# Last attention stage of a 16-batch kernel: scores in two row halves, value masks on ScalarE, and residual additions on GpSimd

## The reference

```
q = norm(x) @ c_Wq + c_bq                  # 256 rows, 16 heads of 8
k = o @ c_Wk + c_bk;  v = o @ c_Wv + c_bv  # o: the 16 slots of the batch
a = softmax(q k^T / sqrt(8))               # for each head: 256 x 16
out = x + (a v) @ c_Wo + c_bo              # heads side by side, then c_Wo
```

## Time and profile before

| | |
|---|---|
| median of 3 runs | 196.59 us (196.57 to 197.86) |
| profiled execution | 196.71 us, its span 195.2 us |
| busy in the span | PE 179.0, DVE 140.9, ACT 118.2, POOL 147.7 us |
| last stage | about 145.6 to 195.2 us |
| granted clock of PE | 1.00 of full |

### The profile page before, as it was taken

How to read it: one execution, slowest core, us unless ns; L and a number is a source line. 1 busy time by engine, 2 the same in 40 slices (tenths; PEclk the granted TensorE clock), 3 DMA queues, 4 the chain that set the end, 5 groups by cost and what they waited for, 6 DMA issues and landing times.

```text
span 195.2 us, 4705 instructions
## 1 busy us (share of the span) xinstructions
PE 179.0 (92%) x1439; PEld 136.3 (70%) x1439; DVE 140.9 (72%) x409; ACT 118.2 (61%) x297; POOL 147.7 (76%) x289
## 2 busy tenths in 40 slices
PE   0588899999999999999999999999977799999994
PEld 0525577778877778777878776623656599999993
DVE  1468978898869786977676652555536999999971
ACT  1323467796889778778767676535412466665661
POOL 4898877899988965969478591306947999999970
PEclk9999999999999999999999999999999999999999
DMA  3749948999980000000000000000000001111122
GB/s 91 240 150 367 349 120 321 331 380 317 382 212 3 0 2 3 3 0 3 0 3 0 2 5 0 3 0 0 3 0 0 3 27 54 57 57 44 42 81 81
DMA packets 19658, 18.24 MB, mean 93 GB/s; under 512 B 1273, under 2 KB 15442, under 8 KB 19634
## 3 DMA queue, kind: packets, MB, share of 16 engines
q1 hardware_dynamic: 18130, 16.76, 26.8%
q10 hardware_dynamic: 1504, 1.18, 1.9%
HBM read 15.84 MB, written 2.10 MB: 92 GB/s over the span
## 4 chain that ended last, share of the span: by engine, by line
PE 82%; DVE 6%; POOL 5%; issue 2%; DMA 1%; ACT 1%; ACTq 1%; DVEq 0%
PE ps L1006 15%; PE ps L1262 7%; PE ps L1076 6%; PE ps L1235 6%; PE ps L1121 4%; PE ps L1179 4%; PE ps L1016 4%; PE ps L1252 4%; PE ps L1109 4%; PE ps L1059 3%; PE ps L1039 3%; PE ps L1243 3%; PE ps L1029 3%; PE ps L1049 2%; PE ps L1068 2%
## 5 line engine op out<-in xcount | busy, mean ns | idle before, releaser
L1006 PE MATMUL ps<-Wproj,xnT 128*128 128x512 f32 x64 | 32.3, 629 | 1.7 <-ACT xnT L559 0.8
L463 POOL TENSOR_TENSOR pr<-ft,rsm 128x256 f32<-128x256 f32 x32 | 19.3, 625 | 0.9 <-DVE rsm L922 0.9
L1006 PEld LDWEIGHTS ps<-Wproj,xnT 128*128 128x128 f32 x64 | 11.5, 199 | 10.7 <-issue 9.4
L1235 PE MATMUL ps<-xnT,XN2T 128*128 128x256 f32 x64 | 16.5, 383 | 1.8 <-POOL xnT L470 1.0
L631 ACT ACTIVATE ft<-ex 128x512 f32<-128x512 f32 x16 | 10.1, 630 | 12.0 <-POOL pr L463 7.1
L1262 PE MATMUL ps<-sq,prT 128*128 128x128 f32 x128 | 16.8, 275 | 0.0
L751 DVE TENSOR_REDUCE ss<-sq 128x64 f32<-128x512 f32 x16 | 10.8, 678 | 8.1 <-ACT sq L535 7.9
L1076 PE MATMUL ps<-XN2T,Ad 128*128 128x256 f32 x64 | 16.6, 382 | 0.0
L411 POOL TENSOR_SCALAR xn<-X,nm,rs 128x127 f32<-128x127 f32 x32 | 14.7, 469 | 1.7
L528 ACT ACTIVATE pr<-ps,nmax 128x256 f32<-128x256 f32 x32 | 14.9, 472 | 1.7 <-DVE nmax L790 1.6
L379 POOL TENSOR_SCALAR xn<-X,nm,rs 128x127 f32<-128x127 f32 x32 | 14.9, 477 | 1.1 <-PE ps L1039 0.9
(11 more groups left out here) (173 smaller groups left out, 510.4 us busy)
## 6 DMA issues: line engine op xcount, KB each, us to landing
W1s<-in_L_ffn_e_W_dram SPq DMA_DIRECT2D x4, 1024.0 KB, 8.2
Wgs<-in_L_ffn_e_Wg_dram SPq DMA_DIRECT2D x4, 1024.0 KB, 8.7
W2s<-in_L_ffn_e_W_dram SPq DMA_DIRECT2D x16, 256.0 KB, 8.3
out_dram<-V2s SPq DMA_DIRECT2D x16, 128.0 KB, 1.7
X<-in_L_attn_x_dram SPq DMA_DIRECT2D x2, 512.0 KB, 6.6
X<-in_L_attn_x_dram ACTq DMA_DIRECT2D x1, 512.0 KB, 7.1
X<-in_L_attn_x_dram ACTq DMA_DIRECT2D x1, 384.0 KB, 5.9
X<-in_L_attn_x_dram ACTq DMA_DIRECT2D x1, 128.0 KB, 2.4
```

Source lines behind the costliest of these rows:

```text
L463: last = pool.tensor_tensor(heads(at[:, k, j * HS:(j + 1) * HS], S), heads(ep[:, k, j * HS:(j + 1) * HS], S), over(rsm[:, k, j * H:(j + 1) ...
L1006: last = pe.matmul(ps[:, j, :], xnT[:, k, j * P:(j + 1) * P], Wproj[:, :], start=True, stop=True)
L1235: last = pe.matmul(ps[:, 2 + k, j * HS:(j + 1) * HS], XN2T[:, b, j * P:(j + 1) * P], BDk[:, k, :], start=True, stop=True)
```

## The change

The masked keys have 128 columns in place of 256: rows 0 to 63 hold heads 0 to 7 and rows 64 to 127 hold heads 8 to 15, in the same columns. The scores of a half of the rows are then two products, each over 64 rows and 128 columns, into two banks, which DVE reads in one view. The four banks of scores leave one for the turned weights, one for the value product (both had two) and two for the output.

The values' mask leaves POOL. ACT reads the value product of all batches out of PSUM once for each head, with the head's column of the mask as scale and the masked bias, and writes that head's columns of BDv for all 16 batches (which lies now in the space of expert weights that are used up). Eight of these 16 instructions stand ahead of `step2`, four behind the exponential of batch 0, four behind that of batch 1. PE waits for all 16 before the first value product.

For the batches 0, 1, 2, 4, 5, 6, 8, 9, 10 and 12 (`BY_POOL`) ACT copies the output from PSUM to `ob` one step after PE made it, between its exponential and its `atT`, and POOL adds the rows, between its `at` and its BDk. The other six stay with DVE. SP waits for POOL's or DVE's semaphore by batch.

```diff
+BANK_TT, BANK_VW, BANK_OUT = 4, 6, (5, 7)
+
+BY_POOL = tuple(int(b % 4 != 3 and b < NB - 3) for b in range(NB))
...
-        BDv = qm[:, :, 0:HS]
+        BDv = W1s[:, 0:8, :].rearrange("p e f -> p (e f)").rearrange("p (b m) -> p b m", b=NB)
...
+        def scored(k):
+
+            return ps[:, 2 * k:2 * k + 2, 0:NT].rearrange("p r (g s) -> p r g s", s=S)
...
             def step2(t):
-                if live(t, 5):
-                    b, k = of(t, 5)
-                    wait(pool, vwp_ok, b - 1)
-                    pool.tensor_tensor(heads(BDv[:, k, :], S), under(vT[:, :, b], H), over(head8[:, :], S),
-                                       ALU.mult).then_inc(bdv_ok, 1)
                 if live(t, 6):
...
                     last.then_inc(at_ok, 1)
+                if live(t, 8) and BY_POOL[t - 8]:
+                    b, k = of(t, 8)
+                    wait(pool, kept_ok, sum(BY_POOL[:b + 1]))
+                    pool.tensor_tensor(ob[:, k, :], ob[:, k, :], X[:, b, :], ALU.add).then_inc(obp_ok, 1)
                 if live(t, 1):
                     b, k = of(t, 1)
                     wait(pool, sp_ok, b - 1)
-                    pool.tensor_tensor(heads(BDk[:, k, :], S), under(kT[:, :, b], H), over(head8[:, :], S),
+                    pool.tensor_tensor(heads(BDk[:, k, 0:P], S), under(kT[:, :, b], H // 2), over(head8c[:, :], S),
                                        ALU.mult).then_inc(bdk_ok, 1)
...
+            def head_values(h):
+
+                sc.activation(BDv[:, :, h * S:(h + 1) * S], ps[:, 5, 0:2 * P].rearrange("p (s b) -> p b s", b=NB),
+                              ACT.Identity, bias=bcv8[:, h:h + 1], scale=head8[:, h:h + 1]).then_inc(bdv_ok, 1)
+
             sc.wait_ge(kvp_ok, 4)
-            sc.activation(vT[:, :, :].rearrange("p s b -> p (s b)"), ps[:, 5, 0:2 * P], ACT.Identity,
-                          bias=vecT[:, BCV:BCV + 1]).then_inc(vT_ok, 1)
+            for h in range(8):
+                head_values(h)
...
                     sc.activation(ep[:, k, :], sx[:, k, :], ACT.Exp).then_inc(ep_ok, 1)
+                    if b < 2:
+                        for h in range(8 + 4 * b, 12 + 4 * b):
+                            head_values(h)
+                if live(t, 7) and BY_POOL[t - 7]:
+                    b, k = of(t, 7)
+                    wait(sc, op_ok, b + 1)
+                    wait(sc, stored[k], (b // 2) * 16, NB * 8)
+                    sc.activation(ob[:, k, :], ps[:, BANK_OUT[k], 0:NT], ACT.Copy).then_inc(kept_ok, 1)
                 if live(t, 5):
...
+                ve.tensor_tensor(head8c[:, :], head8[:, 0:H // 2], head8[:, H // 2:H], ALU.add)
+                ve.tensor_scalar(bcv8[:, :], head8[:, :], vecT[:, BCV:BCV + 1], None, ALU.mult)
...
-                if live(t, 5):
+                if live(t, 5) and not BY_POOL[t - 5]:
...
                     for j in range(2):
-                        last = pe.matmul(ps[:, 2 + k, j * HS:(j + 1) * HS], XN2T[:, b, j * P:(j + 1) * P],
-                                         BDk[:, k, :], start=True, stop=True)
+                        for r in range(2):
+                            rows8 = slice(r * 64, r * 64 + 64)
+                            last = pe.matmul(ps[:, 2 * k + r, j * P:(j + 1) * P], XN2T[rows8, b, j * P:(j + 1) * P],
+                                             BDk[rows8, k, 0:P], start=True, stop=True)
                     last.then_inc(sp_ok, 1)
                 if live(t, 4):
                     b, k = of(t, 4)
-                    wait(pe, bdv_ok, b + 1)
-                    wait(pe, vw_ok, b - 1)
+                    wait(pe, bdv_ok, H)
+                    wait(pe, vw_ok, b)
...
                     wait(pe, at_ok, b + 1)
-                    wait(pe, atT_ok, b - 1)
+                    wait(pe, atT_ok, b)
...
-                    wait(pe, ob_ok, b - 1)
+                    if b >= 2 and BY_POOL[b - 2]:
+                        pe.wait_ge(kept_ok, sum(BY_POOL[:b - 1]))
+                    elif b >= 2:
+                        pe.wait_ge(ob_ok, (b - 1) - sum(BY_POOL[:b - 1]))
```

More of the change, by code:

```diff
@@ L111, in build @@
         head4 = sb("head4", P, EG)
+        head8c = sb("head8c", P, H // 2)
+        bcv8 = sb("bcv8", P, H)
         heads64 = sb("heads64", P, P // 2)
@@ L229, in build @@
         ta_ok, actT_ok, y_ok, o2s_ok, to_ok = (sem(n) for n in ("ta_ok", "actT_ok", "y_ok", "o2s_ok", "to_ok"))
-        o2_ok, kvp_ok, kT_ok, vT_ok = (sem(n) for n in ("o2_ok", "kvp_ok", "kT_ok", "vT_ok"))
+        o2_ok, kvp_ok, kT_ok = (sem(n) for n in ("o2_ok", "kvp_ok", "kT_ok"))
         stored = [sem("stored0"), sem("stored1")]
@@ L291, in _ @@
             for b in range(NB):
-                sp.wait_ge(ob_ok, b + 1)
+                if BY_POOL[b]:
+                    sp.wait_ge(obp_ok, sum(BY_POOL[:b + 1]))
+                else:
+                    sp.wait_ge(ob_ok, b + 1 - sum(BY_POOL[:b + 1]))
                 sp.dma_start(out_rows[:, b, :], ob[:, b % 2, :]).then_inc(stored[b % 2], 16)
@@ L469, in step2 @@
                     wait(pool, sp_ok, b - 1)
-                    pool.tensor_tensor(heads(BDk[:, k, :], S), under(kT[:, :, b], H), over(head8[:, :], S),
+                    pool.tensor_tensor(heads(BDk[:, k, 0:P], S), under(kT[:, :, b], H // 2), over(head8c[:, :], S),
                                        ALU.mult).then_inc(bdk_ok, 1)
             pool.wait_ge(kT_ok, 2)
-            for t in range(STEPS2):
-                if t == 5:
-                    pool.wait_ge(vT_ok, 1)
+            for t in range(STEPS2 + 1):
                 step2(t)
@@ L641, in step2 @@
                     wait(sc, op_ok, b - 1)
-                    sc.activation(VWs[:, k, :], ps[:, 1 - k, 0:HS], ACT.Copy).then_inc(vw_ok, 1)
+                    sc.activation(VWs[:, k, :], ps[:, BANK_VW, 0:HS], ACT.Copy).then_inc(vw_ok, 1)
             for t in range(STEPS2):
@@ L911, in step2 @@
                     wait(ve, ep_ok, b - 1)
-                    ve.tensor_tensor(heads(sx[:, k, :], S), heads(ps[:, 2 + k, :], S), over(mx[:, k, :], S),
-                                     ALU.subtract).then_inc(sx_ok, 1)
+                    ve.tensor_tensor(sx[:, k, :].rearrange("p (r g s) -> p r g s", r=2, s=S), scored(k),
+                                     mx[:, k, :].rearrange("p (r g) -> p r g", r=2).unsqueeze(3)
+                                     .broadcast_to([P, 2, H, S]), ALU.subtract).then_inc(sx_ok, 1)
                 if live(t, 2):
@@ L930, in step2 @@
                     wait(ve, sp_ok, b + 1)
-                    ve.tensor_reduce(mx[:, k, :], heads(ps[:, 2 + k, :], S), AX.X, ALU.max).then_inc(mx_ok, 1)
+                    ve.tensor_reduce(mx[:, k, :].rearrange("p (r g) -> p r g", r=2), scored(k), AX.X,
+                                     ALU.max).then_inc(mx_ok, 1)
             ve.wait_ge(xcbo_ok, NB)
@@ L1239, in step2 @@
                     b, k = of(t, 4)
-                    wait(pe, bdv_ok, b + 1)
-                    wait(pe, vw_ok, b - 1)
+                    wait(pe, bdv_ok, H)
+                    wait(pe, vw_ok, b)
                     for hf in range(2):
-                        last = pe.matmul(ps[:, 1 - k, hf * P:(hf + 1) * P], BDv[:, k, hf * P:(hf + 1) * P],
+                        last = pe.matmul(ps[:, BANK_VW, hf * P:(hf + 1) * P], BDv[:, b, hf * P:(hf + 1) * P],
                                          W[:, CO, :], start=True, stop=True)
@@ L1248, in step2 @@
                     wait(pe, at_ok, b + 1)
-                    wait(pe, atT_ok, b - 1)
+                    wait(pe, atT_ok, b)
                     for j in range(2):
                         for hf in range(2):
-                            last = pe.transpose(ps[:, 4 + k, hf * NT + j * P:hf * NT + (j + 1) * P],
-                                                at[:, k, j * HS + hf * P:j * HS + (hf + 1) * P], ident[:, :])
+                            last = pe.transpose(ps[:, BANK_TT, hf * NT + j * P:hf * NT + (j + 1) * P],
+                                                at[:, k, hf * HS + j * P:hf * HS + (j + 1) * P], ident[:, :])
                     last.then_inc(tt_ok, 1)
```

10 lines of the change are left out of this document (5 added, 5 removed).

## The result

The changed kernel takes 207.73 us (median of 4 runs, 206.63 to 208.9) against 196.99 for the kernel before: a ratio of 1.055 (95% interval 1.050 to 1.060). It is slower, by 10.7 us, and it lies 1.4 us above the top of the forecast range. The executed profile took 208.57 us, with a span of 206.9.

What follows compares the result with a forecast made beforehand. PE bounds the last stage now; a ring of POOL and ACT waits would bound it after. Start, rings and tail put the last weights' end at 196.2 for 189.79: 196.71 + 6.4 = 203.1 us (203.0 against the median), range 200.5 to 206.3.

Steps and rivals of the forecast that it cites:

- The sign: Whole kernel: slower, by +6.4 us; chances slower 0.88, same 0.10, faster 0.02.
- Rival (1): Last stage: PE keeps the pace because the waits have slack; 197.2 us, not measurably slower; chance 0.08.
- The ring: Last stage: POOL's addition waits for ACT's exponential and copy, which wait for POOL's weights; 3.40 us a batch; chance 0.70.
- the start: Stage's beginning: sixteen ACT value masks delay the first value product to 153.2 from 150.34; batch 3's weights end at 162.1.
- The high end of the range: 206.3 us: value masks at 0.474 (+1.1), the circle of waits at 3.55 (+1.35), scores not side by side (+0.9).
- Side by side: PE's 64-row score products run in pairs at once, 0.43 us a batch instead of 0.86 one after the other.
- 0.31 a round trip: PE's scores: entering and leaving the tiled shape costs 0.31 us a batch, making scores 0.74 for 0.86.
- a step of 2.52: PE's time per batch in the last stage, with scores at 0.74: 2.52 us for 2.64.
- The one bank of values: Single value-product bank: costs later steps nothing; the last two batches wait 0.45 us each, 0.9 in the tail.
- its rivals: PE-paced cases charged 0.9 us at the tail: 197.2 us (chance 0.08), or 195.5 with free shape changes (0.05).

Runs made afterwards that it cites:

- e2: Changed kernel with POOL's output addition one POOL step later, behind the next batch's weights; 203.70 us, ratio 1.028.
- e5: Changed kernel with ACT's copy of the output moved ahead of its exponential in the same step; 204.64 us, ratio 1.035.
- e6: Kernel before with only ACT's output copies and POOL's additions for the same ten batches put in; 212.86 us, ratio 1.075.
- e3: Changed kernel with five unused products on PE ahead of its wait for the value masks; 206.28 us, ratio 1.041.
- e10: Scores-only kernel (64-row scores, new banks, half key mask) with the eight score instructions made twice; 203.96 us, ratio 1.029 to the kernel before.
- e4: Changed kernel with values masked per batch by POOL and all additions on DVE, as before; 198.42 us, ratio 0.999 to the kernel before.
- e1: Changed kernel with all sixteen output additions on DVE and no output copy on ACT; 205.31 us, ratio 1.035.
- e9: Changed kernel with POOL's addition one step later and five unused products keeping PE busy before the value masks; 202.03 us, ratio 1.023.
- e7: Kernel before with only ACT's value masks, head by head for all batches, replacing POOL's value mask; 201.09 us, ratio 1.018.
- e8: Scores-only kernel with the value product over 64 rows too, its halves in two banks, one output bank; 198.70 us, ratio 1.006.

## Why the prediction was right in its cause and too low

**The sign and the mechanism held.** Rival (1), PE keeps the pace, is out: POOL's wait is in all ten rounds. The ring was put at 3.40 and is 3.36; piece by piece, the hand-over to ACT is 0.08 (0.08 forecast), exponential to copy 0.54 (0.54), the addition's duration 0.73 (0.73), the key mask's 0.465 (0.47). e2 and e5 open it from either end without moving work between engines, and e6 builds it in the other kernel at the size of the sum. From the end of A(3) to the end of A(15) the profile has 201.54 - 167.06 = 34.5 us, the forecast 34.1.

**What failed is the step called the start.** It said that A(3) would end 16.5 us into the stage (162.1 - 145.6); it ended 19.9 into it (167.06 - 147.15), 3.4 later. Two things made that up.

First, a term that was not in the sum: the clock. The text lets PE wait for the masks until 153.2 and then counts the value product at 0.45 and the scores at 0.74. After 4.65 us without an instruction PE had the level of 1.2 GHz, and they took 1.22 and 1.18. e3 gives its price, 2.3 us: there A(3) ends 17.6 us into the stage. How long the low level lasts behind the wait differs from one execution to the next, so this price does too (e2). The profile before shows a clock of 1.00 in the whole stage; I took that for a property of the stage, and it belonged to a PE that hardly waits.

Secondly, a term that was mis-sized: a value mask takes 0.47 start to start (3.75 for eight), not 0.40. The new instruction lasts longer than the L622 that I took, 0.599 us mean for 0.474:

```profile
L634 ACT ACTIVATE W1s<-ps,bcv,head 128x256 f32<-128x256 f32 x16 | 7.7, 599 | 3.9 <-PE ps L1242 3.9
```

It differs in two things, the scale from memory and the strides, and no run separates them. Over sixteen the value product came 8.48 us into the stage for 7.6, 0.9 late. The two terms make 3.2 of the 3.4 us.

The high end of the range had the masks at 0.474, but nothing for the clock. The rest of the distance is no fault of the mechanism. A(5) to A(7) and A(9) to A(11) took 5.27 each for 5.17, and A(8) to A(9) 3.64 for 3.40 (the exponential waits for DVE there), 0.4 over all steps. And the profiled execution's stage began 1.55 later than that of before, for the most part ahead of the change's first instruction, as said above. The sum, 3.4 + 0.4 + 1.55, is about the 5.5 us between the 208.57 of the profile and the 203.1 forecast for it.

**The scores.** "Side by side" held (e10). "0.31 a round trip" was too small: it is 0.42, and with 0.44 for the products the two terms add up to the 0.86 of before, so this part of the change gains nothing (e4: ratio 0.999). I had said 0.12 a batch, a step of 2.52 for PE where e1 has 2.64. In the changed kernel the ring hides the difference. The Trainium skill says in "TensorEngine Tiling (Array Packing)", Key Properties, that changing the tiling mode drains TensorE. The trace agrees, with about 0.2 us for each change of shape.

**The one bank of values** costs the steady steps nothing, as said. For each of the last two batches it costs 0.6 of waiting rather than 0.45, and the value product takes 0.23 more, 1.7 us in all where the text had 0.9 (e4). The text charged it to its rivals only; in the changed kernel the ring hides it.

**The sum as the runs have it.** The two parts of the stage (us, one profile each):

| kernel | first part | second part |
|---|---|---|
| before | 11.77 | 34.97 |
| changed | 16.26 | 40.68 |
| e1, no additions on POOL | 16.48 | 36.65 |
| e2, additions late | 15.60 | 36.64 |
| e3, PE kept busy | 13.98 | 40.70 |
| e4, scores and banks alone | 10.45 | 36.64 |
| e9, e2 and e3 together | 14.00 | 36.65 |

Of 10.2 us the ring is 4.0 (40.68 - 36.65), the half clock 2.3 (16.26 - 13.98), the later value product, less what the shorter masks and scores give back, 2.2 (14.00 - 11.77), and the one bank at the end 1.7 (36.65 - 34.97). The first two are what taking them away gives. The other two are what e9 is left with, and e4, which has the one bank but not the value masks, shows the last by itself. It shows only when the ring is gone, which hides it as long as it stands. Four kernels without the ring agree in the second part to 0.01 us, so these differences are no scatter. The first part scatters more, with the length of the low clock.

## What to carry to other kernels

An engine can be relieved on paper and still set the end: before moving an operation, write down the order on both engines and follow each wait once around; if the way back leads through another engine's instruction that waits for the first one, the sum of that circle is the step, not the load. Here the shift of one instruction past its neighbour, on either engine, took 3.8 to 4.0 us off.

One producer that makes a thing for all batches at once moves its whole time ahead of the first consumer. Where PE waits for that, count its clock as well: here gaps of 3.6 us (e7) and of 4.65 us (the changed kernel) without an instruction were followed by 3.5 to 6.5 us of work at the low level.

Splitting products into tiles would have paid here only with more of them side by side in one place: each change of shape took 0.2 us, as much as four products of 64 x 128, and eight of them gained just what the two changes cost.

## What the runs showed of the hardware

- TensorE had no instruction for 4.65 us and ran at the 1.2 GHz level for the next 6 us, although it was busy without a gap again. In the profiles of e1, e2, e5 and e7, which have such a wait too, the low level lasted 3.5 to 6.5 us behind it. e3 shows the full level throughout when ten unused instructions fill the wait.
- 64-row products of 128 columns in fp32 run two at a time: 0.055 us for each further one (e10), against 0.11 for one over 128 rows. Changes to and from that shape took 0.21 us each at the full clock.
- Four 64-row value products behind eight 64-row score products took 0.47 us, no less than four whole ones (e8). The cause was not settled.
- ACT's instruction with scale and bias from memory, 256 elements, strided in source and target: 0.60 us long and 0.47 start to start, where the one with the bias alone was 0.47 long (L622) and the plain copy 0.38 (L642).
